# Context order and FFN front put together: statistics ahead, spread by one matmul, GpSimd on the sigmoids of three chunks and one chunk of the product

## What is computed

```python
x = x + xattn_0(layernorm(x), ctx)        # attention with distances over 257 keys
x = x + attn_0(layernorm(x))              # "ratio" attention: dot*dot / (|q|^2 + |k|^2 - 2 dot)
x = x + ffn_0(layernorm(x))               # the quantised FFN, below
x = x + xattn_1(layernorm(x), ctx)        # "context" attention: one head, 257 keys
x = x + attn_1(layernorm(x))              # segments
x = x + ffn_1(layernorm(x))               # 8 experts

def act_qdq(x):                           # 16 bits, one scale for the whole tensor
    scale = jnp.maximum(jnp.max(jnp.abs(x)) / 32767., 1e-12)
    return jnp.clip(jnp.round(x / scale), -32768., 32767.) * scale
def ffn_0(x):
    x = act_qdq(x)
    up = act_qdq(x @ dequant(w_up).T)     # 1024 x 768
    gate = act_qdq(x @ dequant(w_gate).T)
    sig = jnp.clip(jnp.round(sigmoid(gate) * 65536.), 0., 65535.) / 65536.
    gate = act_qdq(gate * sig)
    o = act_qdq(gate * up)
    return o @ dequant(w_down).T
def xattn_1(image, text):
    q, k, v = image @ Wq.T + bq, text @ Wk.T + bk, text @ Wv.T + bv
    return softmax(q @ k.T / 16.) @ v
```

## Time and profile before

| what | us |
|---|---|
| median of 3 runs (707.36 to 707.98) | 707.64 |
| the profiled execution | 707.23 |
| its span, first to last instruction | 705.4 |
| TensorE busy in the span | 621.6 (88%) |
| VectorE busy | 460.2 (65%) |
| ScalarE busy | 366.2 (52%) |
| GpSimd busy | 315.3 (45%) |

### The profile page before, as it was taken

The page is one execution under the profiler, slowest core; times in us unless marked ns, Lnnn a source line. Parts: engine busy times, 40 slices in busy tenths (PEclk is TensorE's granted clock), DMA queues, the critical chain, the costliest instruction groups (busy, mean ns, idle before and its releaser), DMA issues.

```text
span 705.4 us, 18761 instructions
## 1 busy us (share of the span) xinstructions
PE 621.6 (88%) x7075; PEld 476.0 (67%) x7075; DVE 460.2 (65%) x1279; ACT 366.2 (52%) x992; POOL 315.3 (45%) x458
## 2 busy tenths in 40 slices
PE   4999999999999999769947999989999758999990
PEld 3787888788877787534425876568888545777760
DVE  1797777777776898844888835478999873333320
ACT  1665666565656898643945634356665521222220
POOL 1346666666652898300000212075756414656641
PEclk9999999999999999969966999999999978999995
DMA  8833233333300000293001447075020032444434
GB/s 268 264 107 89 81 76 92 85 77 84 89 5 3 4 4 4 55 341 113 0 0 45 195 180 291 10 303 221 4 69 2 2 106 56 67 66 64 62 39 73
DMA packets 31704, 65.20 MB, mean 92 GB/s; under 512 B 5792, under 2 KB 21792, under 8 KB 29312
## 3 DMA queue, kind: packets, MB, share of 16 engines
q1 hardware_dynamic: 26016, 55.73, 24.0%
q0 software_dynamic: 4688, 7.18, 6.5%
q10 hardware_dynamic: 912, 1.10, 0.5%
HBM read 57.67 MB, written 7.37 MB: 92 GB/s over the span
## 4 chain that ended last, share of the span: by engine, by line
PE 64%; DVE 21%; ACT 3%; issue 3%; DMA 2%; SPq 2%; POOL 1%; DVEq 0%; ACTq 0%; POOLq 0%
PE psum L2648 8%; PE psum L491 7%; PE psum L499 7%; PE psum L2658 4%; PE psum L529 4%; PE psum L1502 3%; PE psum L1479 3%; PE psum L868 3%; DVE ff_peak L1520 2%; PE psum L515 2%; PE psum L544 2%; PE psum L859 2%; PE psum L851 2%; PE psum L899 2%; DMA wn<-in_w_down 2%
## 5 line engine op out<-in xcount | busy, mean ns | idle before, releaser
L802 POOL TENSOR_SCALAR bias<-dist,cst 128x257 f32<-128x257 f32 x128 | 61.1, 496 | 74.8 <-issue 43.0
L491 PE MATMUL psum<-ctxT,shared 128*128 128x257 f32 x256 | 65.9, 401 | 2.3 <-DMA msk<-in_mask 2.2
L424 ACT ACTIVATE prob<-s_sb,negm 128x257 f32<-128x257 f32 x128 | 64.9, 509 | 1.0 <-DVE negm L665 0.9
L499 PE MATMUL psum<-shared,ctxT 128*128 128x256 f32 x256 | 60.8, 380 | 0.0
L661 DVE CUSTOM_DVE_ANT_0 s_sb<-psum,bias 128x257 f32<-128x257 f32 x128 | 46.6, 421 | 20.0 <-PE psum L515 17.1
L1741 POOL TENSOR_TENSOR wn<-wn,cst 128x1 f32<-128x1 f32 x8 | 4.7, 588 | 122.7 <-DVE wn L1868 122.7
L2648 PE MATMUL psum<-ex_w,shared 128*128 x184 | 58.3, 460 | 0.6 <-ACT shared L2541 0.6
L491 PEld LDWEIGHTS psum<-ctxT,shared 128*128 128x128 f32 x256 | 47.1, 194 | 12.5 <-issue 4.9
L413 ACT COPY kT<-psum 128x257 f32<-128x257 f32 x64 | 24.0, 374 | 60.3 <-PE psum L491 60.3
L499 PEld LDWEIGHTS psum<-shared,ctxT 128*128 128x128 f32 x256 | 46.5, 191 | 5.1
L2648 PEld LDWEIGHTS psum<-ex_w,shared 128*128 128x128 f32 x184 | 33.1, 190 | 15.4 <-issue 0.8
(11 more groups left out here) (357 smaller groups left out, 1610.9 us busy)
## 6 DMA issues: line engine op xcount, KB each, us to landing
ctxT<-in_ctx_T SPq DMA_DIRECT2D x32, 257.0 KB
ex_w<-in_w SPq DMA_DIRECT2D x1, 5632.0 KB, 17.2
kpos<-in_kpos SPq DMA_DIRECT2D x32, 128.5 KB
msk<-in_mask SPq DMA_DIRECT2D x32, 128.5 KB
near_turned<-in_ctx_T_tiles SPq DMA_DIRECT2D x4, 1028.0 KB
ff_used_up<-in_ctx_T_tiles SPq DMA_DIRECT2D x4, 1028.0 KB
near_rows<-in_ctx_tiles SPq DMA_DIRECT2D x4, 1024.0 KB, 8.0
ff_used_up<-in_ctx_tiles SPq DMA_DIRECT2D x4, 1024.0 KB, 7.7
```

Of the source, the lines that this page charges most:

```text
L424: nc.scalar.activation(prob[n % 2][:, g, :], s_sb[n % 2][:, g, :], ACT.Exp, bias=negm[:, b, g:g + 1], accum_out=esum[t % 2][:, b, g:g + 1]) \
L491: ins = nc.tensor.matmul(kv[m][:, 0:SK], w["xa_k"][:, k, P * m:P * m + P], ctxT[n % BT][:, k, :], start=(k == 0), stop=(k == KT - 1))
L499: ins = nc.tensor.matmul(kv[0][:, D * i:D * i + D], ctxT[n % BT][:, k, P * i:P * i + P], w["xa_v"][:, k, :], start=(i == 0 and k == 0), st ...
L802: nc.gpsimd.tensor_scalar(bias[n % 2][:, g, :], dist[n % 2][:], c.slope[:, g:g + 1], 1.0 / FAR, ALU.mult, ALU.mult).then_inc(bias_ready, 1)
```

## The change

It changes the order of instructions and their engine at seven places, and nothing of what is computed.

1. A new class `NormAhead` holds statistics, variance, root and shift (minus mean times root) of the FFN's norm. Statistics of tile 0, 1 and 2, 3, 4 are taken in ratio steps 3, 4, 5, 6 on VectorE; GpSimd makes the root of the five and five shifts of 128x1 in step 6. Tiles 5 and 6 follow inside the last ratio step, tile 7 reads its statistics from PSUM. GpSimd normalises tiles 0 to 2, ScalarE 3 to 6, VectorE 7.
2. `spread_top` is one matmul, of the column broadcast to 128x128 with the identity; VectorE then takes the maximum over 128 columns on every partition. This holds for all five scales.
3. `context.pe_fold` (which waits for all of the context's weights) stands on TensorE behind the last ratio output and ahead of `spread_top(X)`; its copy `context.act_start` stands on ScalarE behind the last ratio output. The fold of the segments stands ahead of `spread_top(U)`. The first group of gate matmuls but one waits for the context's copy.
4. x is rounded by VectorE (pairs 0 and 2) and ScalarE (pairs 1 and 3).
5. The first gate chunk goes through the sigmoid loop in halves of 512 tokens, its integers made by VectorE. The sigmoids of chunks 1, 2 and 4 are rounded and clipped by GpSimd (L1429 and L1432), that of chunk 5 by two activations of ScalarE; chunks 0 and 3 stay on VectorE.
6. VectorE makes the integers of gate chunk 0 behind the scale of h. GpSimd makes the product of chunk 1 with both roundings (L1436 twice, L1439). VectorE goes through chunks 0, 2, 3, 1, 4, 5, and makes half of the integers of the first quarter of o.
7. Context: `context.pe(pe, t - 7)` behind down tile t from 4. The key bias is a product of xn and a row (`key_row`, 128x256) with an accumulated sum on VectorE, and a 128x1 addition. y comes first in a step and one step later, GpSimd adds the value bias before it makes the root; ScalarE's exponential stands ahead of the copy of xT.

```diff
@@ class NormAhead @@
+    EARLY = 5
+    TILES = {3: (0,), 4: (1, 2), 5: (3,), 6: (4,)}
@@ spread of a maximum @@
         def spread_top(i):
             pe.wait_ge(top_ready, i + 1)
-            nc.tensor.transpose(turned_top, top[:, i:i + 1], c.ident).then_inc(top_turned, 1)
-            pe.wait_ge(most_ready, i + 1)
-            nc.tensor.matmul(topall, ones[0:1, :], most[0:1, i:i + 1], start=True, stop=True,
-                             skip_group_check=True).then_inc(topall_full, 1)
+            nc.tensor.matmul(every_top, top[:, i:i + 1].broadcast_to([P, P]), c.ident, start=True, stop=True,
+                             skip_group_check=True).then_inc(top_spread, 1)
@@ GpSimd @@
+        for i, m in enumerate(CLIPPED_BY_POOL):          # (1, 2, 4)
+            pool.wait_ge(sig_ready, m + 2)
+            nc.gpsimd.tensor_scalar(sig[:, m % 2, :], sig[:, m % 2, :], 1.0, 192.0, ALU.mult, ALU.add) \
+                .then_inc(sig_clipped, 1)
+            pool.wait_ge(sig_clipped, 2 * i + 1)
+            nc.gpsimd.tensor_scalar(sig[:, m % 2, :], sig[:, m % 2, :], 192.0 + LARGEST, 192.0, ALU.min, ALU.max) \
+                .then_inc(sig_clipped, 1)
+        for ready, n, piece in ((up_1, MADE_BY_POOL + 1, up), (h_1, MADE_BY_POOL, gate)):
+            pool.wait_ge(ready, n)
+            nc.gpsimd.tensor_scalar(piece[:, MADE_BY_POOL, :], piece[:, MADE_BY_POOL, :], -ROUND, 1.0, ALU.add, ALU.mult) \
+                .then_inc(product_made, 1)
+        pool.wait_ge(product_made, 2)
+        nc.gpsimd.tensor_tensor(gate[:, MADE_BY_POOL, :], gate[:, MADE_BY_POOL, :], up[:, MADE_BY_POOL, :], ALU.mult) \
+            .then_inc(product_made, 1)
@@ TensorE, ahead of the scale of x @@
+        ratio.pe_features(pe, NT - 1)
+        context.pe_fold(pe)
         pe.wait_ge(wt_done, 9)
@@ TensorE, down and context @@
-            if 2 <= t < NT - 2:
-                context.pe(pe, t - 5)
+            if t == 4:
+                pe.wait_ge(context.consts_done, 1)
+                pe.wait_ge(segment.row_ready, 1)
+            if t >= 4:
+                context.pe(pe, t - 7)
@@ VectorE, key bias @@
+        def key_bias(dve, n):
+            dve.wait_ge(xn_ready, n + 1)
+            st.link(dve, nc.vector.scalar_tensor_tensor(
+                bias_wide[:].rearrange("p k t -> p (k t)"), xn[n % 2][:], SCALE, key_row[:], ALU.mult, ALU.mult,
+                accum_out=qb[:, n:n + 1]))
+            st.link(dve, nc.vector.tensor_scalar(qb[:, n:n + 1], qb[:, n:n + 1], offset[:], None, ALU.add))
```

More of the change, by code:

```diff
@@ L205, in ffn_and_context @@
             quantised_ffn(nc, block, given_back, a, lambda name, shape, dt=F32: sb(name, shape, dt, till_context), second_sem, bank, c, x, w, loaded,
-                          wn, cx[0], ratio[0], Region(shared), segment[0])
+                          wn, cx[0], ratio[0], Region(shared), segment[0], ahead)
         def segments(block):
@@ new lines, in _ @@
+        dve.wait_ge(ratio.y_full, NT)
+        nc.vector.bn_stats(ahead.stats[:, LAST, :], ratio.y_part).then_inc(y_seen, 1)
+        dve.wait_ge(y_seen, 1)
+        ahead.aggregate(LAST)
+        ahead.variance(dve, LAST, NT)
+        dve.wait_ge(ahead.rstd_ready, 3)
+        dve.wait_ge(ratio.y_done, NT)
+        st.link(dve, nc.vector.tensor_scalar(xn[:, LAST, :], x[:, LAST, :], mv[:, LAST, 0:1], rstd[:, LAST:NT],
+                                             ALU.subtract, ALU.mult))
+        st.link(dve, magnitude(X, 2, xn[:, LAST, :]))
@@ L1835, in pe_step @@
                 ins.then_inc(p_full, 1)
+            if there(u + 2):
+                n = u + 2
+                pe.wait_ge(xT_done, n + 1)
+                at_least(pe, k_done, n)
+                for m in range(KT):
+                    for k in range(KT):
+                        ins = nc.tensor.matmul(k_bank[:, P * m:P * m + P], fold[:, k, P * m:P * m + P],
+                                               xT[n % 2][:, k, :], start=(m == 0 and k == 0), stop=True,
+                                               skip_group_check=True)
+                ins.then_inc(k_full, 1)
             if there(u + 1):
@@ L2012, in pool_step @@
                 ins.then_inc(kbd_ready, 1)
+            if root_due and u < 0:
+                root(pool, t + 3)
             if s == 1 and there(t + 1):
```

470 lines of the change are left out of this document (287 added, 183 removed).

## The result

The changed kernel takes 698.31 us (median of 4 runs, 696.75 to 699.52), the kernel before 707.50 in the runs beside it (705.44 to 707.98). The ratio is 0.9868, with a 95% interval of 0.984 to 0.9895: 1.3% faster, 9.2 us. It lies where rival B put it (698.3), which is luck: B's reasons are only half of what happened, and its terms were not met one by one. The table follows the span.

A forecast was written before the change was run, and what follows sets the result against it. The prediction took TensorE and VectorE, in different stages, to bound the kernel. Its terms, 0.8 + 0.75 - 0.4 - 4.9 = -3.75 us, applied to the median of 707.64, gave 703.9 us, range 699.5 to 707.6.

The forecast's parts named there:

- rival B: GpSimd and VectorE don't exclude each other, or GpSimd's instructions are near 1.1 us: 698.3 us, chance 0.2.
- Views and bound: Whole kernel: TensorE (64% of the chain of waits) and VectorE (21%) matter, in different stages.
- tX: Time the inverse scale of x is set: 1.7 us later, as the context fold delays the spread on TensorE.
- tX to tG: From the inverse scale of x to that of gate: 0.6 and 0.3 us less, by shared rounding and a shorter spread.
- Loop: Sigmoid loop, from the inverse scale of gate to that of h: +0.75 us, at 1.5 us per GpSimd pass.
- The shared port: VectorE's products and 128x1024 roundings and GpSimd's long instructions probably exclude each other: 2.8 us lost in the sigmoid loop.
- Product: From the inverse scale of h to that of o: -0.4 us (-3.2 to +2.0).
- Context: Down and context stage, from the inverse scale of o to the last segment step's start: -4.9 us (-2.7 to -6).
- rival E: Context stage: VectorE's chain holds each tile and only half of the 4.9 us comes: 706.3 us, chance 0.1.
- Behind: From the segments' first product of probabilities and values to the end of the span: no change, 0 us.
- C: Ratio tail: the context fold holds nothing up, x's inverse scale comes 2.8 us earlier: 699.4 us, chance 0.08.
- D: GpSimd becomes the bound, from about 1.85 us per instruction, and the kernel is slower: 709.3 us, chance 0.1.

The follow-up runs named there:

- the first experiment: The changed kernel with the second GpSimd pass over the sigmoids of chunks 1, 2 and 4 done twice; ratio 0.9937 to the kernel before.
- clip_234: The changed kernel with the fold in the sigmoid loop, chunk 1's product on VectorE, and GpSimd clipping chunks 2, 3, 4; 695.86 us, ratio 0.983.

## Why the prediction was wrong, step by step

Two terms failed. The price of a GpSimd pass was put at 1.5 us and is 1.04, and with it the wait for chunk 1 and the time in which GpSimd blocks VectorE were put too high: 1.8 and 2.8 us in the loop, where 0.99 and 1.17 were measured, and 2.8 in the product, where it was 1.6. This is how loop and product gained 1.8 and 1.1 us more than forecast. And the order of the matmuls in a context step was put at nothing, while it brings 0.34 us in each step that has scores, y and mix, some 2 us. The first two stretches gained 1.0 more than forecast, and the part behind, put at 0, gave 1.65 back. The profiles thus differ by 8.0 us where 3.75 was forecast; that the medians differ by 9.2 lies within the scatter of the executions.

**Views and bound.** Right. VectorE in the loop and TensorE in the context steps were the two engines from which a gain arrives in full.

**tX.** Right in mechanism and nearly in size: +1.2 for +1.7. The fold waits for the last weight, runs at clock 0.50, and holds the spread. The part I gave without it, 2.8 us earlier, was too much: with the fold away it was 1.3 us earlier than before (304.62). It left out the tail's own 0.5, which was 0.63 (VectorE's last transposition of the ratio began at 293.33, before at 292.70). And it had struck out the long maximum: in the kernel with the fold away VectorE still waits 0.78 us for ScalarE's normalised tiles and takes a maximum of 1.22 us before it comes to tile 7.

**tX to tG.** -1.4 for -0.9. The granted clock in this stretch was 0.94 where it had been 0.88 from 305.9 to 335.9 before, a thing that I had not put into the sum. It is the turning of x: from tX to the first gate matmul the clock was 0.78 where it had been 0.50, since TensorE had just worked on the fold, and that took 4.33 us for 5.43; from there on it was 0.97 in both. The stretch varies: it took 27.17 to 29.55 us in the kernels above.

**Loop.** -1.0 for +0.75. The failed step is the price of a GpSimd pass, "I take 1.5, the middle": it is 1.04, under my lower end of 1.11, because I drew the slope through the smallest 128x1 row. From 476 ns for 257 columns to 1,040 for 1,024 it is 0.735 ns a column. That gave the wait for chunk 1 (0.99 for 1.8) and the collisions (0.76, and 0.41 at the inverse of h, for 2.8). In the other direction, the H spread saved 0.2 and not 0.6: its one matmul takes 0.81 us in the chain where the old first one took 0.37, and VectorE waits 0.89 us for it. The Trainium skill (GPSIMD Engine Reference, section 3.1) has two figures, 1.8 cycles per element in the best case and 1.03 where the ports bound the loop, "for k ≤ 2", which I read as at most two operations per element; the prediction set only the first beside its price. By the second, an estimate for 1,024 elements at 1.2 GHz is 0.88 us and a fixed part, and the 1.04 us of the rows are near it; the 0.735 ns a column between the two rows are below its 0.86.

**The shared port.** Right, and now shown from both sides: with GpSimd's instructions away the stretched rows fall back to 1.22 and 0.15 us. That VectorE's long roundings are caught as well shows on GpSimd's side in the first experiment, where a pass beside a rounding of 0.68 us took 1.42. I had taken only long instructions to be caught; the 128x1 TENSOR_TENSORs of the inverse and the unit are caught as well, for 0.41 and 0.65 us on the path. By the lock of the Trainium skill (SBUF — State Buffer, section "SBUF: two separate sides"), which speaks of two SBUF inputs and of no size, they would be.

**Product.** -1.5 for -0.4: here the price of the product was right (2.36 for 2.3) and GpSimd's two passes were shorter. Half of its 5.3 us was said to fall on VectorE, 2.8; it was 2.0, of which 0.4 before tH. The O spread saved 0.15 and not 0.6.

**Context.** -6.9 for -4.9. The key bias was right to the hundredth, 0.34 per tile. Missing was that the order of the groups has a price: some 0.34 us per step, over the six steps that have scores, y and mix an estimate of 2 us. 0.14 of it is shown to hang on whether scores and mix, which use 32 columns of the array, stand together or have y on 128 columns between them (1.91 for 2.05 us). That the other 0.2, in the turnings, is the same price is only argued. VectorE, with 10.6 of 17.8 us, was not the bound, so rival E falls.

By the mark that the -4.9 was made for, the step gained more and then lost some. The segment step's first matmul of 8 columns (L2294, before L2120) began at 447.16 where it had been 458.89, which from tO is 9.0 us less. Up to the segments' first product 2.1 of them are lost: the y of tile 7 now stands there, and TensorE waits 2.18 us until VectorE has added it. I had put its return at +0.7:

```profile
454.12 0.58 PE L2299 MATMUL psum<-late,shared 128*128 128x8 f32 x4 [2.18 <-DVE x L2062]
```

**Behind.** +1.65 for 0. The marks go -9.65 at the first segment product, -9.6 at the last matmul of the routing (573.24 for 582.83), -8.0 at the end. Most of the last part is the clock ahead of the experts, where three matmuls of no use but for the clock run: the first expert's matmuls come 6.7 us behind the last matmul of the routing, before 5.3. Window and rows of that place, before and then after:

```profile
583.00:588.00 5.00, 4.53 (x12) 1.89 (x9) 2.45 (x13) 0.37 (x1) 3.18 (x4) 0.70 0.21 54
```

```profile
573.50:579.00 5.50, 5.50 (x11) 2.19 (x8) 2.45 (x13) 0.00 (x0) 3.76 (x4) 0.50 0.24 58
573.40 5.47 PE L846 MATMUL psum<-ex_w,cst 128*128 128x512 f32 x6
```

They took 5.47 us in six profiles and 4.06 to 4.32 in five of kernels that have the same code there, four of these with the change, so the change does not fix which it is. What does is open.

**Range and rivals.** B's time is met, and its condition "near 1.1 us" too, but with the exclusion present; its loop (-2.05) and product (-3.2) were both larger than measured (-1.0 and -1.5), and the context's extra 2.0 made up for them: that the sum fits is luck. C, D and E did not happen. The low end of the range left out half of B, with a chance of 0.2, and nothing of the context's gain beyond -6.

## What to carry to other kernels

Before handing work to GpSimd beside a VectorE that multiplies two tensors, write down on which VectorE instructions its passes will fall: beside a reduction they cost nothing (1.21 us as without one), while a product waits for the rest of the pass. Here a change of one tuple, from chunks 1, 2, 4 to 2, 3, 4, was worth 2.0 us in the loop, three times what GpSimd's help was worth in the first arrangement, though the whole time (0.983 for 0.9832) does not show it. A filler such as a fold belongs where its engine idles and no load is awaited. And group the matmuls of a step by the columns of the array that they use, but look first for a ring of buffers that an order closes: here the ring cost 1.05 us a step, and the change of columns 0.14 for one pair.

## What the runs showed of the hardware

- A GpSimd TENSOR_SCALAR of 128x1024 with two operations took 1.04 us, a TENSOR_TENSOR 2.36.
- A VectorE TENSOR_TENSOR of 128x1 waited for a running GpSimd pass as a large one does: 0.57 and 0.80 us for 0.16 and 0.15. A TENSOR_REDUCE of 128x1024 did not: 1.21 us beside a pass.
- Two groups of sixteen matmuls on 32 columns of the array took 1.91 us one behind the other, and 2.05 with matmuls on 128 columns between them.
- Matmuls of no use, moved from behind to ahead of an idle time of 2.09 us, did not bring the granted clock up for what followed: the expert matmuls took 4.58 us at 0.55, for 2.63 at 1.00.
- The best kernel of this study, clip_234, has 0.983 of the time of the kernel before; that it is better than the changed one (0.9868) rests on intervals that just overlap, 0.9813 to 0.9847 and 0.984 to 0.9895.
